# Graph network, two node-sum stages: sums accumulated in PSUM at register addresses, one broadcast comparison per group

## The reference

```
deg = segment_sum(ones, dst) + 1
norm = rsqrt(deg)[src] * rsqrt(deg)[dst]
conv(h, W, b): h = h @ W
               agg = segment_sum(h[src] * norm[:, None], dst)
               return agg + h / deg[:, None] + b
x = relu(conv(conv(x, W1, b1), W2, b2))
```

## Time and profile before

| | |
|---|---|
| runs | 42078.96, 42104.45 and 42115.75 us; median 42104.45 us |
| span of the profiled execution | 42291.0 us (the page gives no own time beside it) |
| busy in the span | PE 30086.1 us (71%), PEld 18136.7 (43%), DVE 29025.3 (69%), ACT 11308.4 (27%), POOL 30957.5 (73%) |
| stage l2a, l2b | about 13.25 to 15.83 ms and 15.90 to 18.48 ms |
| stage l3m, six times | from 18.6 ms on |
| queue of the gathers | 669696 packets, 495.09 MB, 7.9% of 16 engines |

### The profile page before, as it was taken

How to read it: one execution, slowest core, us unless ns; L and a number is a source line. 1 busy time by engine, 2 the same in 40 slices (tenths; PEclk the granted TensorE clock), 3 DMA queues, 4 the chain that set the end, 5 groups by cost and what they waited for, 6 DMA issues and landing times. The chain is left out here.

```text
span 42291.0 us, 514812 instructions
## 1 busy us (share of the span) xinstructions
PE 30086.1 (71%) x99425; PEld 18136.7 (43%) x99426; DVE 29025.3 (69%) x63440; ACT 11308.4 (27%) x26426; POOL 30957.5 (73%) x31499
## 2 busy tenths in 40 slices
PE   5222234444465232359999999999999999999999
PEld 5332323333355332334444444444444444444444
DVE  7333322221155222259999999999999999999999
ACT  0000001111120000024444444444444444444444
POOL 1665655555523666669998998899899989998997
PEclk8555556655565555579999999999999999999999
DMA  1110012221131010011111111111111111111111
GB/s 46 41 41 24 20 31 62 59 40 21 20 80 24 13 12 13 12 29 45 46 45 44 46 46 42 47 46 45 44 45 46 45 44 46 45 46 43 46 45 42
DMA packets 1365881, 1670.85 MB, mean 40 GB/s; under 512 B 847196, under 2 KB 1012047, under 8 KB 1252303
## 3 DMA queue, kind: packets, MB, share of 16 engines
q1 hardware_dynamic: 664232, 1115.69, 8.1%
q0 software_dynamic: 669696, 495.09, 7.9%
q10 hardware_dynamic: 31680, 57.69, 0.4%
HBM read 1393.98 MB, written 274.47 MB: 39 GB/s over the span
## 5 line engine op out<-in xcount | busy, mean ns | idle before, releaser
L1808 PE MATMUL l3m_p_w<-en,l3m_hid 128*128 128x512 f32 x42240 | 20965.0, 619 | 653.2 <-issue 298.7
L1858 DVE TENSOR_REDUCE l3m_xg<-l3m_prod 128x32 f32<-128x1024 f32 x10560 | 12850.4, 1217 | 189.9
L1730 POOL DMA_INDIRECT l3m_xg<-wide_table,l3m_mt x10560 | 10340.7, 979 | 2427.4 <-issue 2262.8
L1739 POOL TENSOR_TENSOR l3m_prod<-l3m_rest,l3m_xg 128x384 f32<-128x384 f32 x10560 | 10674.3, 1011 | 279.8 <-ACT l3m_rest L1785 93.6
L1808 PEld LDWEIGHTS l3m_p_w<-en,l3m_hid 128*128 128x128 f32 x42240 | 7164.7, 189 | 6867.5 <-issue 5443.1
L1785 ACT COPY l3m_rest<-l3m_p_w 128x384 f32<-128x384 f32 x10560 | 5050.5, 478 | 12801.6 <-PE l3m_p_w L1808 11967.6
L1870 DVE TENSOR_TENSOR l3m_prod<-l3m_p_w,l3m_xg 128x512 f32<-128x512 f32 x10560 | 7185.8, 680 | 422.9 <-PE l3m_p_w L1808 247.4
L1820 PEld LDWEIGHTS l3m_p_sum<-l3m_xg,l3m_apart 128*125 128x125 f32 x21120 | 3965.6, 188 | 5090.2 <-issue 2741.4
L1773 ACT ACTIVATE l3m_apart<-iota_lo,l3m_mt 128x125 f32<-128x125 f32 x10560 | 4239.0, 402 | 15.3 <-issue 14.1
L1820 PE MATMUL l3m_p_sum<-l3m_xg,l3m_apart 128*125 128x64 f32 x21120 | 3474.4, 246 | 22.6 <-DVE l3m_xg L1858 22.6
L837 POOL DMA_INDIRECT l2a_xg<-table,l2a_mt x1760 | 1675.4, 952 | 2087.7 <-DMA l2a_mt<-dst_meta 1240.1
(11 more groups left out here) (328 smaller groups left out, 22398.8 us busy)
## 6 DMA issues: line engine op xcount, KB each, us to landing
l3m_hid<-hid_t SPq DMA_DIRECT2D x660, 1024.0 KB
l3m_xg<-wide_table,l3m_mt POOLq DMA_INDIRECT x10560
hid_t<-l_hid SPq DMA_DIRECT2D x110, 1024.0 KB, 4.1
order_src_bk<-dst_bucket SPq DMA_DIRECT2D x52, 808.0 KB
order_dst_bk<-src_bucket SPq DMA_DIRECT2D x52, 808.0 KB
by_dst<-order_src_empty SPq DMA_DIRECT2D x28, 1071.0 KB, 24.5
l_rec<-by_dst SPq DMA_DIRECT2D x110, 272.0 KB, 3.7
l_xg<-table,l_mt POOLq DMA_INDIRECT x1760
```

The costliest lines, as they stand in the source:

```text
L1730: pool.indirect_dma_start(xg[s][:, j, 0:2 * D], None, wide_table[:, :], bass.IndirectOffsetOnAxis(ap=mt[s][:, j, 0:1].bitcast(I32), axis=0 ...
L1739: pool.tensor_tensor(o_i(prod[j % RING][:, OWN:HD]), o_i(rest[j % RING][:, :]), state_of(s, j, REST), ALU.mult).then_inc(pooled, 1)
L1808: ins = pe.matmul(p_w[j % 2][:, c * 512:(c + 1) * 512], hid[s][:, j * P:(j + 1) * P], en2[:, c * 512:(c + 1) * 512], start=True, stop=True)
L1858: dve.tensor_reduce(xg[s][:, j, 2 * D:3 * D], o_i(prod[j % RING][:, :]), AX, ALU.add).then_inc(msgs, 1)
```

## The change

Both stages get a PSUM tile of 128x3584 (seven banks), `p_acc`, in place of five tiles of 128x512. VectorE clears it once at the start, and TensorE waits for that once. TensorE loads the 16 columns of a group into registers of its own and accumulates each product at its bucket's columns in `p_acc` for the whole stage (start=False). The waits for `added` and the adds are gone. VectorE makes all 16 matrices of a group by one tensor_tensor comparison, both operands broadcast; after the last group it copies 125x3200 of `p_acc` to `ACC`. `row_regs` are the registers that l1a uses. SP's and GpSimd's code is the same.

```
+        SUMW = -(-W // 512) * 512
...
-                p_sum = [ph.ps(f"p_sum{s}", [P, 512]) for s in range(NBUF)]
+                p_acc = ph.ps("p_acc", [P, SUMW])
...
-                hits, summed, added, begun = (ph.sem(n) for n in ("hits", "summed", "added", "begun"))
+                hits, summed, cleared, begun = (ph.sem(n) for n in ("hits", "summed", "cleared", "begun"))
...
                     @block.vector
                     def _(dve):
-                        def find(i, s):
-                            dve.wait_ge(meta_in[s], i * 16 + 16)
-
-                            dve.wait_ge(summed, i * NBUF + (s + 1))
-                            for j in range(G):
-                                ins = dve.tensor_scalar(hit[s][:, j, :], iota_lo[:, :], mt[s][:, j, 1:2],
-                                                        None, ALU.is_equal)
-                            ins.then_inc(hits, 1)
-
-                        def add(i, s):
-                            add_sums(dve, added, summed, p_sum, off, acc, i * NBUF + s, s, NBUF)
-
-                        dve.sem_inc(added, NBUF * G)
-                        for s in range(NBUF - 1):
-                            find(0, s)
-                        with dve.Fori(0, NG // NBUF - 1) as i:
+                        wide = [P, G, LO]
+                        dve.memset(p_acc[:, :], 0.0).then_inc(cleared, 1)
+                        with dve.Fori(0, NG // NBUF) as i:
                             for s in range(NBUF):
-                                if s:
-                                    find(i + 1, s - 1)
-                                else:
-                                    find(i, NBUF - 1)
-                                add(i, s)
-                        find(NG // NBUF - 1, NBUF - 1)
-                        for s in range(NBUF):
-                            add(NG // NBUF - 1, s)
+                                dve.wait_ge(meta_in[s], i * 16 + 16)
+
+                                dve.wait_ge(summed, i * NBUF + (s + 1))
+                                dve.tensor_tensor(hit[s][:, :, :], iota_lo[:, None, :].broadcast_to(wide),
+                                                  mt[s][:, :, 1:2].broadcast_to(wide), ALU.is_equal).then_inc(hits, 1)
+
+                        dve.wait_ge(summed, NG + NBUF)
+                        dve.tensor_copy(acc[:, :], p_acc[0:LO, 0:W])
 
                     @block.tensor
                     def _(pe):
                         pe.sem_inc(summed, NBUF)
+                        pe.wait_ge(cleared, 1)
                         with pe.Fori(0, NG // NBUF) as i:
                             for s in range(NBUF):
-                                pe.wait_ge(hits, i * NBUF + (s + 1))
+                                g = i * NBUF + s
+                                pe.load(row_regs, off[0:1, bass.ds(g * G, G)])
+                                pe.wait_ge(hits, g + 1)
                                 pe.wait_ge(rows_in[s], i * (16 * G) + 16 * G)
-
-                                pe.wait_ge(added, (i * NBUF + s) * G + G)
                                 for j in range(G):
-                                    ins = pe.matmul(p_sum[s][0:LO, j * D:(j + 1) * D], hit[s][:, j, :], xg[s][:, j, :],
-                                                    start=True, stop=True)
+                                    at = pe.snap(row_regs[j], min_val=0, max_val=W - D)
+                                    ins = pe.matmul(p_acc[0:LO, bass.ds(at, D)], hit[s][:, j, :], xg[s][:, j, :],
+                                                    start=False, stop=True, skip_group_check=True)
                                 ins.then_inc(summed, 1)
```

## The result

The changed kernel takes 42163.86 us (median of 20 runs, 42150.98 to 42193.08), the kernel before 42102.13 us (20 runs): a ratio of 1.0015, 95% interval 1.0009 to 1.0022, 62 us slower. The forecast was 41975 us, 130 us faster.

The account below looks back on a forecast made before the run. It took GpSimd's gathers in l2a and l2b, waiting 635 us on late TensorE, as the pace. Waits -459, register operations +380, stage ends -51 gave -130 us: 42104.45 to about 41975 us, range 41600 to 42450.

Parts of the forecast that it names:

- The named waits go: 459 us less.: l2a and l2b: TensorE's waits for VectorE's adds and comparisons disappear, 459 us less; bounds 0 and 635.
- theory N: From the experiments, l2a and l2b: GpSimd's waits belong to the gather stream itself, whatever TensorE issues; 300 to 330 us per stage.
- rival (e): l2a and l2b: waits only renamed, TensorE spends them on slow issue; about -51 us, 42053 us; chance 0.12.
- (c): l2a and l2b: GpSimd never waits, the hold-up still counts; -362 us, 41742 us; chance 0.20.
- (d): l2a and l2b: GpSimd never waits and no gather is held up; -714 us, 41390 us; chance 0.05.
- 380 us for slow register operations.: TensorE in l2a and l2b: 15% of register operations take 0.70 us, adding 380 us in both; bounds 0 and 760.
- The hold-up: 1.6 us, 352 us in both stages.: l2a and l2b: the two-SBUF-input comparison delays one gather per group, 1.6 us on average, 352 us on GpSimd.
- They count 0 in the sum.: l2a and l2b: GpSimd's 635 us of waits absorb the 352 us hold-up, so it adds nothing to the total.
- rival (a): l2a and l2b: comparison holds up gathers and nothing pays for it; +273 us, 42377 us; chance 0.23.
- The end of a stage: 25.5 us less.: Ends of l2a and l2b: without adds, one PSUM copy follows the last matmul; 25.5 us earlier, 51 us in both.
- (1): Sign in l2a and l2b: no named TensorE wait for VectorE; GpSimd's sum waits well under 320 us per stage.
- (4): Sign at a stage's end: the last gather is followed by about 31 us instead of 56.6.

Follow-up runs that it names:

- sixteen comparisons: Changed kernel with 16 tensor_scalar comparisons per group instead of one tensor_tensor: ratio 1.0000 without waits; 42191.24 us against 42252.51 for before on a chip with waits.
- row of places in PSUM: Changed kernel whose broadcast comparison reads the row of places from a PSUM copy, one input in SBUF: ratio 0.9991 without waits, 0.9982 with.
- chips with waits: Chips where GpSimd waits for sums in l2a and l2b; the unchanged kernel before took 42253 to 42298 us on three.
- fixed columns: Changed kernel without TensorE's register load and register operations, products at fixed PSUM columns: 39929.68 us, ratio 1.0074, on a chip without waits.
- kernel with one product: Kernel with the row of places in PSUM, one of 16 products per group kept: 42006.80 us on a chip with waits, 39534.61 on one without.
- doubled comparison: Changed kernel making the broadcast comparison twice per group, second time into a spare tile: 42410.41 us against 42267.74 for before, with waits.
- chip without waits: Chip where GpSimd never waits for sums in l2a; the unchanged kernel before took 39570 to 39635 us on three.
- before with the same comparison: Kernel before with only the broadcast comparison in place of its 16, additions kept: ratio 1.0086 without waits; 42269.99 us against 42297.94 with.
- the first comparison: First measurement of the changed kernel against before, 20 runs each: 42163.86 against 42102.13 us, ratio 1.0015.

## Why the forecast was wrong

**"The named waits go: 459 us less."** This is the step that failed. The waits did go by name, and with sixteen comparisons, where only the first gather of a stage is held, the first to the last gather fell from 2523 to 2510 us in l2a and from 2521 or 2525 to 2511 in l2b: 10 to 14 us per stage, not 230. With the row of places in PSUM it is 2507 and 2505. What went as waits came back as TensorE's issue, 1744 us instead of 1407 in l2a. TensorE's waits for VectorE were not what set GpSimd's pace, and a wait by name is not time that is won when its cause is taken away. I had read GpSimd's waits as TensorE being late, because what is waited for is a sum; by theory N they were the form in which a limit on the stream of gathers came out. That is rival (e)'s picture, and (c) and (d) did not come about on chips with waits for the same reason. One of the two signs of being wrong that I had named came true in these kernels: GpSimd's waits stayed (302 us in l2a, 40 of them) although TensorE waited for VectorE nowhere.

**"380 us for slow register operations."** Failed too, in the other direction: all of TensorE's take 44 to 50 ns, although VectorE's take 700 in such stretches; taking them out saved 3 to 8 us per stage. The share behind the term was also read too simply: I divided all of issue by 2.59 us and got 543 slow matmuls, where the trace has 572 idle times before matmuls, of which 382 are 2.5 us or longer. Two errors of 459 and 380 us nearly cancelled, and the -79 left of them looked like a small term. That 42164 us lies within the range of 41600 to 42450 is owed to this cancelling, and is luck.

**"The hold-up: 1.6 us, 352 us in both stages."** Right. 1.50 us on chips with waits, 165 us per stage, and 1.65 us without, 181 us per stage (1.54 us with fixed columns); mean gather 1038 ns where I wrote 1.04 us, the comparison 2.242 us where I wrote 2.24.

The Trainium skill (SBUF — State Buffer, Who interferes with whom) states that a VectorE instruction with at most one SBUF input, outside the 2-port perf modes, does not contend with GpSimd. By that rule the copy in PSUM frees the gathers, and the trace agrees: no gather over 962 ns in the runs with 16 products, on either kind of chip. The longer gathers of the kernel with one product are the other kind's own, since most of them run beside no VectorE instruction. The Trainium skill's remark in the same section that tensor_tensor was not seen to stall a DMA is not borne out for these gathers: in the changed kernel 110 gathers per stage, one per comparison, were held.

**"They count 0 in the sum."** Partly wrong. On the one chip where both kernels were profiled, of 150 us of longer gathers in l2a 122 were paid from waits and 34 were not (with 5 us more issue). I had asked only whether GpSimd's own path, 2359 us, stays below 2523. It did, and yet a part came through, as it did with the doubled comparison (own path 1908 + 532 = 2440, stage 2623). On a chip without waits nothing is paid and rival (a)'s mechanism is the result, 336 us where (a) had 273, mostly because the end of a stage gives back 2 us there and not 25.5. The bound "0 to 493" held both; the sum took its lower end. Why the changed kernel pays more of the hold-up (34 us) than before with the same comparison (11 us) is not settled. In the latter 99 gathers of l2a are held, not 110; the end of the stage gives back 8 of the 23 us between them.

**The end of a stage: 25.5 us less.** Measured 21.5 us in the first comparison; 24.0 us on the chip where both were profiled (56.6 against 32.6). Without waits it is 2 us: there the additions kept up with the gathers. The memset takes 3.05 us and is hidden, as forecast.

**What would show it.** (1) came true in both halves; (2) did not, no slow register operation; (3) and (4) came true (held gathers up to 3.0 us, the first of the stage 3.9; 35.1 us for 31); (5) failed: l3m moved by 37 us and the stages before l2a by 174, with their code unchanged. The sum for such a chip by what was measured: -13 for the additions, -24 at the end and +39 to +47 for the hold-up (2549 and 2557 against 2510), so +2 to +10 us per stage, where 5 (3 in l2b) and 10 (14 in l2b) were found. It is a sum made after the result, of parts from several chips.

**The better kernel** is the one that keeps the sums in PSUM and reads the row of places from PSUM: 0.9991 (0.9982 to 1.0000) without waits, which is not clear of no change, and 0.9982 (0.9973 to 0.9991) with them, against 1.0085 and 1.0005 to 1.0015 of the change.

## What to carry to other kernels

When an engine waits for a result, price the gain by what the waiting engine would do if the result were there at once, and look for a limit in its own stream before the waits are counted as a fund: here they shrank from 308 to 274 us when the late engine's work was cut by half. A wide comparison with both inputs in SBUF costs the gather that starts beside it about its remaining length; with one operand in PSUM the same instruction held up none. And compare kernels on one chip only, with the untouched stages as a check on what differs for no reason of the change.

## What was not expected of the hardware

- Six chips, the same kernel: 39570 to 39635 us on three, 42253 to 42298 on the other three (42102 in the first comparison). Between two profiles of before, 42291.0 and 39573.5 us, the two edited stages differ by 311 and 313 us from first to last gather and the stages before them by 2048 us; l3m, with a gather every 2.16 us instead of every 1.25 to 1.43, is the same on both. The clock is not the difference: the granted clock of TensorE is 0.50 (its level of 1.2 GHz) throughout l2a in both profiles.
- On the slower kind the trace has no landing times for these gathers, and on the others it has 2.4 us. What is short on the slower kind was not found, and whether the recording of the trace itself has a share in it was not tried.
- On the slower kind VectorE's register operations take 0.7 us in stretches and TensorE's matmuls have 2.6 us before them, but TensorE's register operations never exceed 50 ns.
- l3m's message stage takes 3797 to 3798, 3800 or 3803 us by the loading of the program, with a mean gather of 979 to 980, 981 or 982 ns; both extremes came with the unchanged kernel too, and with the one kernel with one product. What differs between the loadings was not tried.
